# A graph network's edge loop: the bias laid into PSUM by ScalarE, half of the one-hot matrices made on GpSimd, and a new order of the stages

## The reference

```
h    = relu(layernorm(x))                        # 3125 x 256
ei   = concat([h[src], edge_attr])               # 50000 x (256 + 64)
core = relu(ei @ W1 + b1) @ W2 + b2              # W1: 320 x 256, W2: 256 x 256
gate = sigmoid(ei @ Wg + bg)                     # Wg: 320 x 256
msg  = gate * core                               # 50000 x 256
agg  = segment_sum(msg, dst, 3125)
x    = x + layernorm(agg + h) * gamma + beta
```

## Time and profile before

| | |
|---|---|
| median of three runs | 1698.13 us (1695.11 to 1700.46) |
| span of the profiled execution | 1691.9 us |
| busy: TensorE matmul, weight load | 1511.9 us (89%), 1378.6 us (81%) |
| busy: VectorE, ScalarE, GpSimd | 1469.6 us (87%), 1202.7 us (71%), 1036.2 us (61%) |
| DMA | mean 188 GB/s |

### The profile page before, as it was taken

The page is one execution under the profiler, slowest core; times in us unless marked ns, Lnnn a source line. Parts: engine busy times, 40 slices in busy tenths (PEclk is TensorE's granted clock), DMA queues, the critical chain, the costliest instruction groups (busy, mean ns, idle before and its releaser), DMA issues. The chain is left out here.

```text
span 1691.9 us, 40433 instructions
## 1 busy us (share of the span) xinstructions
PE 1511.9 (89%) x10735; PEld 1378.6 (81%) x10735; DVE 1469.6 (87%) x3257; ACT 1202.7 (71%) x2896; POOL 1036.2 (61%) x1093
## 2 busy tenths in 40 slices
PE   6879999999999999999669688999998999999874
PEld 3669999999999999999459567787787887777653
DVE  4559999999999999999577689999999999999866
ACT  1458888888888888888056367777776767777573
POOL 0446666666666666664176577777777777777316
PEclk9989999999999999999979899999999999999888
DMA  4356666666666666665125787777777777777813
GB/s 135 138 184 186 187 186 186 186 187 186 187 187 188 185 188 185 187 184 145 33 82 191 221 245 220 231 228 231 227 228 224 225 229 227 229 226 223 281 46 97
DMA packets 164893, 318.92 MB, mean 188 GB/s; under 512 B 30231, under 2 KB 103928, under 8 KB 164436
## 3 DMA queue, kind: packets, MB, share of 16 engines
q0 software_dynamic: 66560, 219.06, 44.8%
q1 hardware_dynamic: 98132, 97.49, 18.7%
HBM read 291.90 MB, written 24.53 MB: 187 GB/s over the span
## 5 line engine op out<-in xcount | busy, mean ns | idle before, releaser
L493 POOL DMA_INDIRECT gath<-edge_in_tab,idx x392 | 413.6, 1055 | 270.5 <-DVE gate_in L933 207.6
L1226 PE MATMUL bank<-weighted,hot 128*128 128x260 f32 x880 | 238.6, 395 | 30.7 <-ACT hot L749 29.6
L506 POOL DMA_INDIRECT kept_more<-kv_tab,idx x176 | 195.5, 1111 | 60.6 <-issue 39.3
L1226 PE MATMUL bank<-w_lo,relu_hi 128*128 128x256 f32 x784 | 221.8, 283 | 0.0
L1226 PE MATMUL bank<-w_hi,relu_lo 128*128 128x256 f32 x784 | 221.7, 283 | 0.0
L1226 PE MATMUL bank<-w_hi,relu_hi 128*128 128x256 f32 x784 | 221.1, 282 | 0.0
L1226 PEld LDWEIGHTS bank<-weighted,hot 128*128 128x128 f32 x880 | 153.2, 192 | 53.4 <-ACT hot L749 36.7
L644 ACT ACTIVATE relu_hi<-bank 128x512 fp32r<-128x512 f32 x196 | 117.4, 599 | 81.4 <-PE bank L1226 81.4
L506 POOL DMA_INDIRECT hs<-kv_tab,idx x132 | 148.1, 1122 | 41.3 <-issue 36.3
L506 POOL DMA_INDIRECT xs<-kv_tab,idx x132 | 141.0, 1068 | 48.7 <-issue 22.7
L1229 PE MATMUL bank<-ident,gath 128*128 128x128 f32 x784 | 150.1, 273 | 10.6 <-DMA gath<-edge_in_tab,idx 10.6
(11 more groups left out here) (284 smaller groups left out, 4924.4 us busy)
## 6 DMA issues: line engine op xcount, KB each, us to landing
block_row<-row_tab SPq DMA_DIRECT2D x440, 64.0 KB
ea_in<-in_ea SPq DMA_DIRECT2D x392, 64.0 KB, 2.4
edge_in_tab<-node_row SPq DMA_DIRECT2D x26, 256.0 KB, 2.0
kv_tab<-qkv_row SPq DMA_DIRECT2D x25, 258.0 KB, 2.5
gath<-edge_in_tab,idx POOLq DMA_INDIRECT x392
xs<-in_x SPq DMA_DIRECT2D x1, 3328.0 KB, 15.2
v_in<-kv_tab SPq DMA_DIRECT2D x25, 130.0 KB, 2.1
rows_tab<-hs SPq DMA_DIRECT2D x25, 128.0 KB, 2.4
```

Source lines behind the costliest of these rows:

```text
L493: g.indirect_dma_start(gath[:, q, i, :], None, edge_in_tab, bass.IndirectOffsetOnAxis(ap=idx[:, half, q, i:i + 1], axis=0)).then_inc(gath_ ...
L506: g.indirect_dma_start(kept(u, 0, KVW)[:, i, :], None, kv_tab, bass.IndirectOffsetOnAxis(ap=idx1[:, half, u % BATCH, i:i + 1], axis=0)).th ...
L1226: return nc.tensor.matmul(out_, lhsT=lhs, rhs=rhs, start=start, stop=stop)
```

## The change

1. b2 is loaded as `b2_rows`, 128 partitions of two copies. A new ScalarE stage `seed` copies it into the bank of `core`; `core` has 12 products instead of 14, all of which accumulate.
2. The one-hot matrices of odd blocks are made on GpSimd by `odd_one_hot`, with an is-equal. ScalarE makes those of even blocks.
3. GpSimd's gathers are written out for all chunks, with the indices straight from `src_chunk`; `idx` and its copy go.
4. VectorE's order: `low_relu`, `add_gate`, `message`, `low_edges`, `low_message`, `add_sums`; lags of sums and low messages are one more, on TensorE too. On ScalarE `gates` is ahead of `high_message`.
5. `split_edges` and `low_edges` work on two chunks at a time, in even steps; `load_edges` waits accordingly. The gate's products wait for `gate_added`.
6. In the prologue, semaphores are merged (same waits), b2's split goes, and one load is added.

```diff
@@ sync
-            sp.dma_start(b2_sb[:], b2.to_broadcast([2 * SHARES, HID])).then_inc(w_in, 16)
+            for i in range(2):
+                sp.dma_start(b2_rows[:, i, :], b2.to_broadcast([P, HID])).then_inc(w_in, 16)
...
-                after(sp, ea_lo_done, c - SLOTS + 1)
+                after(sp, ea_lo_done, (c - SLOTS) // 2 + 1)
@@ gpsimd
+            def gather_node_rows(c):
+                after(pool, gate_added, c - SLOTS + 1)
                 for i in range(2):
+                    g.indirect_dma_start(gath[:, c % SLOTS, i, :], None, edge_in_tab,
+                                         bass.IndirectOffsetOnAxis(ap=src_chunk[:, c, i:i + 1], axis=0)).then_inc(gath_in[c % SLOTS], 16)
+            def odd_one_hot(b):
+                if b % 2 == 1:
+                    after(pool, sum_ready, b - 1)
+                    for i in range(2):
+                        last = g.tensor_scalar(hot[:, 1, i, :], iota_node[:], rel_col[:, b, i:i + 1], None, ALU.is_equal)
+                    last.then_inc(pool_hot_done, 1)
...
+            chunks_and_blocks(pool, [(gather_node_rows, 0, CHUNKS), (odd_one_hot, 4, CHUNKS)])
@@ scalar
             def split_edges(c):
+                if c % 2:
+                    return
...
+                act.wait_ge(ea_arrived[slot + 1], 32 * (c // SLOTS + 1))
+                after(act, z_ready, c + 1 - SLOTS + 1)
+                after(act, gate_ready, c + 1 - SLOTS + 1)
+                s.copy(ea_parts[:, slot:slot + 2, :], ea_in[:, slot:slot + 2, :]).then_inc(ea_hi_done, 1)
...
+            def seed(n):
+                if n < 2:
+                    act.wait_ge(row_ready, WPAD)
+                after(act, msg_done, n - 1)
+                s.copy(bank[4 + n % 2][:], b2_rows[:].rearrange("p i f -> p (i f)")).then_inc(seeded, 1)
             chunks_and_blocks(act, [(split_edges, 0, CHUNKS), (one_hot, 4, CHUNKS), (distances, 3, CHUNKS), (relu_inner, 2, CHUNKS),
-                                    (high_message, 4, CHUNKS), (gates, 3, CHUNKS)])
+                                    (gates, 3, CHUNKS), (high_message, 4, CHUNKS), (seed, 2, CHUNKS)])
@@ vector
             def low_edges(c):
+                if c % 2:
+                    return
...
+                both = slice(slot, slot + 2)
+                v.tensor_tensor(ea_parts[rows, both, :], ea_in[rows, both, :], ea_parts[rows, both, :], ALU.subtract).then_inc(ea_lo_done, 1)
...
-            chunks_and_blocks(dve, [(message, 3, CHUNKS), (low_relu, 2, CHUNKS), (add_gate, 2, CHUNKS), (low_edges, 0, CHUNKS),
-                                    (low_message, 3, BLOCKS), (add_sums, 4, BLOCKS)])
+            chunks_and_blocks(dve, [(low_relu, 2, CHUNKS), (add_gate, 2, CHUNKS), (message, 3, CHUNKS), (low_edges, 0, CHUNKS),
+                                    (low_message, 4, BLOCKS), (add_sums, 5, BLOCKS)])
@@ tensor
             def edge_inputs(c):
...
+                after(pe, gate_added, c - 1)
...
             def core(n):
+                pe.wait_ge(seeded, n + 1)
                 pe.wait_ge(relu_lo_done, n + 1)
                 for i in range(2):
-                    mm(to, share[:], b2_parts[:], True, False)
...
-            chunks_and_blocks(pe, [(edge_inputs, 0, CHUNKS), (sum_messages, 3, BLOCKS), (core, 1, CHUNKS)])
+            chunks_and_blocks(pe, [(edge_inputs, 0, CHUNKS), (sum_messages, 4, BLOCKS), (core, 1, CHUNKS)])
```

More of the change, by code:

```diff
@@ L48 @@
 assert MID[-1] == WINDOWS
[L49 removed]
+assert CHUNKS % 2 == 0 and CHUNKS % (2 * SLOTS) == SLOTS and MSGS % SLOTS == 0 and MSGS > LATE + 4 and BLOCKS % KEEP == 0 and KEEP % BROWS == 0
 def build(nc, x, src, dst, etype, ea, w1, wg, b_cat, w2, b2, ln0, query_col, wqkv, b_qkv, rel, wo, b_o, ln1, out):
@@ L657, in distances @@
             def distances(b):
[L659 to L662, removed]
-            def one_hot(b):
-                act.wait_ge(dist_done, b + 1)
-                after(act, sum_ready, b - 1)
-                s.activation(hot[:, b % 2, :, :], dist[:, b % 2, :, :], ACT.Relu, bias=one_col[:], scale=-1.0).then_inc(hot_done, 1)
+                if b % 2 == 0:
+                    after(act, hot_done, b // 2)
+                    for i in range(2):
+                        last = s.activation(dist[:, i, :], iota_node[:], ACT.Square, bias=rel_col[:, ds(b, 1), i], scale=-1.0)
+                    last.then_inc(dist_done, 1)
+            def one_hot(b):
+                if b % 2 == 0:
+                    act.wait_ge(dist_done, b // 2 + 1)
+                    after(act, sum_ready, b - 1)
+                    s.activation(hot[:, 0, :, :], dist[:], ACT.Relu, bias=one_col[:], scale=-1.0).then_inc(hot_done, 1)
+            def seed(n):
[3 more added lines that the diff above has]
+                s.copy(bank[4 + n % 2][:], b2_rows[:].rearrange("p i f -> p (i f)")).then_inc(seeded, 1)
             chunks_and_blocks(act, [(split_edges, 0, CHUNKS), (one_hot, 4, CHUNKS), (distances, 3, CHUNKS), (relu_inner, 2, CHUNKS),
-                                    (high_message, 4, CHUNKS), (gates, 3, CHUNKS)])
+                                    (gates, 3, CHUNKS), (high_message, 4, CHUNKS), (seed, 2, CHUNKS)])
             act.wait_ge(lw_in, 3 * 16)
@@ L918, in low_edges @@
             def low_edges(c):
+                if c % 2:
+                    return
                 slot = c % SLOTS
-                dve.wait_ge(ea_hi_done, c + 1)
+                dve.wait_ge(ea_hi_done, c // 2 + 1)
                 rows = slice(EDGE_DIM, 2 * EDGE_DIM)
-                v.tensor_tensor(ea_parts[rows, slot, :], ea_in[rows, slot, :], ea_parts[rows, slot, :], ALU.subtract).then_inc(ea_lo_done, 1)
+                both = slice(slot, slot + 2)
+                v.tensor_tensor(ea_parts[rows, both, :], ea_in[rows, both, :], ea_parts[rows, both, :], ALU.subtract).then_inc(ea_lo_done, 1)
             def low_relu(c):
@@ L1242, in _ @@
                 last = mm(bank[2][0:1, 0:BLOCKS], ones_c[0:HALF_C, 0:1], chosen[:, c, :], c == 0, c == 1)
-            last.then_inc(rows_ready, 1)
-            pe.wait_ge(off_ready, 1)
+            last.then_inc(tallies_made, 1)
+            pe.wait_ge(lists_made, 4)
             for i in range(2):
@@ L1269, in _ @@
                     last = mm(bank[3][0:HALF_B, cols], chosen[:, c, some], nat_f[:, 2, c, :], c == 0, c == 1)
-            last.then_inc(cols_ready, 1)
+            last.then_inc(tallies_made, 1)
             pe.wait_ge(meta_ready, 1)
-            pe.wait_ge(w_in, 9 * 16)
+            pe.wait_ge(w_in, 10 * 16)
             def transpose_rows(rows, source_done, freed, ready):
@@ L1325, in edge_inputs, with onto @@
                 last.then_inc(gate_ready, 1)
+            def onto(out_, lhs, rhs):
+                return nc.tensor.matmul(out_, lhsT=lhs, rhs=rhs, start=False, stop=False, skip_group_check=True)
             def core(n):
+                pe.wait_ge(seeded, n + 1)
                 pe.wait_ge(relu_lo_done, n + 1)
@@ L1349, in sum_messages @@
                 pe.wait_ge(msg_lo_done, b + 1)
-                pe.wait_ge(hot_done, b + 1)
+                if b % 2 == 0:
+                    pe.wait_ge(hot_done, b // 2 + 1)
+                else:
+                    pe.wait_ge(pool_hot_done, b // 2 + 1)
                 to = bank[6 + b % 2][:, 0:HID]
```

67 lines of the change are left out of this document (23 added, 44 removed).

## The result

The changed kernel takes 1644.51 us, median of four runs (1641.24 to 1649.24); beside it on the same chip the kernel before takes 1696.72 (1695.11 to 1700.46). The ratio is 0.9698, 95% interval 0.9682 to 0.9713: 52 us faster.

What follows compares the result with a forecast made beforehand. TensorE was taken to bound the first layer's loop: 192 x 0.238 = 45.7 us saved, less 1 for drain and 1 for stalls, 43.7. Span 1648.2 plus 6.2 gave 1654.4 us, range 1647 to 1682.

Steps and rivals of the forecast that it cites:

- What bounds, and the bias: First layer's loop: TensorE bounds; two bias products fewer save 0.238 us a chunk, 45.7 us over 192 chunks.
- Less 1 for the drain, and 1 for small stalls.: Taken off the 45.7 us saving: 1 us for one more step to drain, 1 us for small stalls, leaving 43.7.
- the floor of 3.29: TensorE's least time per chunk in the loop after the change, 3.29 us from 3.53; it set the range's end, 1647.
- No instruction goes; I count 0, and it is what lets 0.238 come through.: VectorE's low relu first, later sums: saves 0 itself, but longer cover for waits lets the bias saving through.
- the ring: VectorE's old order ties W2 stage, message, low relu and next W2 stage together; the change was to free low relu.
- The lead-in: GpSimd's delay before a gather behind a compare: at worst 0.99 us in the open, expected to be prepared during compares.
- rival 1: GpSimd becomes the bound, mildly: 6.7 to 6.9 us per two chunks, 1674 us; chance 0.16, including 0.03 for no change.
- Rival 4: GpSimd's compares and serial lead-ins make the kernel slower: 3.99 us a chunk, 1786 us, or 1700 and up; chance 0.07.
- The loop over the landings: Sum, odd one-hot, next gathers and their landing on GpSimd: 7.85 us against 8.03 available, so it just fits.
- Rivals 3 and 5: TensorE's waits exposed, 0.05 to 0.10 us a chunk, 1664 to 1674 us, chance 0.05; late bias copy, 1680, chance 0.04.
- Ports: GpSimd compares hold up VectorE's two-input SBUF instructions: 0.1 us per two chunks taken; as bound 1659 to 1674, chance 0.10.
- Split for two: VectorE's low split every second chunk: steps of 2.75 and 3.58 us, mean 3.17 in place of 3.31.

Runs made afterwards that it cites:

- Experiment 5: The changed kernel with b2 laid down by two products per chunk again, without ScalarE's copy into PSUM: 1690.28 us, ratio 0.9969.
- experiment 2: The kernel before with VectorE's new order and the later sums alone, ScalarE's order as before: 1691.04 us, ratio 0.9976.
- changed: The changed kernel, with the whole change against the kernel before: 1644.51 us, ratio 0.9698.
- experiment 11: The changed kernel with VectorE's order and lags, TensorE's sums and ScalarE's order as in the kernel before: 1671.57 us, ratio 0.9855.
- two repeats: The changed kernel run again twice, unaltered: 1646.03 us, ratio 0.9709, and 1646.05 us, ratio 0.9696.
- experiment 3: The changed kernel with the message ahead of low relu on VectorE again, lags kept: 1673.7 us, ratio 0.9865.
- experiment 10: The changed kernel, low relu still first, but low messages, hs adds and sums at the lags of the kernel before: 1777.72 us, ratio 1.0477.
- experiments 7 and 8: The changed kernel without GpSimd's compares after the first odd block: 1648.12 us; with one more, unread compare per odd block: 1715.19 us.
- experiment 4: The changed kernel with the edge features split one chunk at a time again, on ScalarE and VectorE: 1650.86 us, ratio 0.9729.

## Why the forecast was right in its mechanism and short in its size

**What bounds, and the bias.** Right. TensorE bounds before and after. The term was 192 x 0.238 = 45.7 us; measured, 195 x 0.230 = 44.9. Experiment 5 gives 0.227 for the two products.

**"Less 1 for the drain, and 1 for small stalls."** This step failed. It took a stretch that TensorE fills to 100% as free of stalls, and allowed for new ones. But a busy share by unions doesn't show them. The starts of the transposes do: a chunk of 3.69 in every eight, so that the mean is 3.55 and not the 3.53 read from one chunk. The order took those in (experiment 2), so the sign was wrong: 3.9 us gained, not 1 lost. The drain cost 0.0 in sum. By itself it does cost what was forecast: the tail is 0.8 us longer with the later sums in experiment 2 than in the kernel before, and 0.9 longer in changed than in experiment 11 (single executions; the tails of changed's two repeats lie within 0.3 of the first). Something else in the change gave that back, and no run shows what. Together 5.9 of the 9.2 us by which 43.7 fell short of 52.9. The range's lower end, 1647, rested on the floor of 3.29, and this held (3.300); it had no room for a kernel before that ran slower than 3.53.

**The rest of the miss.** The first five chunks gained 1.1 us more than the period explains (the order alone has that too: 15.9 us in experiment 2 against 17.1), the first transposes came 0.8 late, and 3.7 us lie behind the first layer, where executions of the same kernel differ by as much. With the term of the bias (-0.8) and those 5.9: 5.9 - 0.8 + 1.1 - 0.8 + 3.7 = 9.1. The time missed by 9.9, as the median lies 5.5 us above the profiled span here and was taken 6.2 above it. What lies behind the first layer and ahead of the loop, 2.9 of the miss, is luck, good or bad. The two repeats, at 1646.0, lie under the range too.

**"No instruction goes; I count 0, and it is what lets 0.238 come through."** The second half is right and the first half was not worked out. Without the order 25 of the 50 us are gone (experiment 11). The working compared VectorE's mean need, 3.17, with 3.29. It is the long step, 3.64 (forecast 3.58), together with what holds up the short one that had to be compared with 6.6: the ring, 3.18, in experiment 3, the wait for the high message and the register load, 3.21 on average, in experiment 11. A rival "the steps don't average" was missing. The edit also has two halves that are only good together: low relu first without the later low message makes changed 5% slower than the kernel before (experiment 10).

**GpSimd.** Two errors that partly cancelled, which is luck. The compare was taken at 0.47; alone it takes 0.61, beside VectorE's two-input instructions 0.80. The lead-in behind it was feared at up to 0.99; it is 0.16, as "the sequencer can prepare the gather" said. 6.59 per two chunks against the 6.3 taken and 6.58 available: rival 1 missed by a hair, and experiments 7 and 8 show how close it was. Rival 4 needed lead-ins of 0.99 in the open, and none came. The loop over the landings, forecast to "just fit", did: TensorE waits for no gather from 200 to 700 us.

**ScalarE.** 2.99 a chunk forecast, 2.84 measured; the copy into PSUM has a pitch of 0.52 (402.64 to 403.16), taken at 0.53. Busy near 90% was forecast, 86% is in the profile. Rivals 3 and 5, waits in the open: no such wait in the trace, and the W2 starts are 0.120 apart against 0.119.

**Ports.** The forecast put the cost on VectorE, 0.1 us of 6.43, and had the compares fall beside the low relu and the gate addition. That place was wrong. VectorE pays 0.07: the low message takes 0.75 in steps with a compare beside it and 0.68 in the others. GpSimd pays more. In changed all 152 compares from 200 to 700 us overlap a low split or low message, mean 0.80; in experiment 10 all 125 lie beside other instructions:

```profile
L491 POOL TENSOR_SCALAR hot<-iota_node,rel_col 128x128 fp32r<-128x128 f32 x125 | 75.5, 616 | 2.1
```

0.19 each, 0.38 us of the 6.60. Being beside one another isn't all of it: in experiment 5 71 compares run 0.5 us beside a low message and take 0.61, and in experiment 3 some take up to 1.17. What makes the difference stays open. The rule of the Trainium skill (GPSIMD Engine Reference, section Specifications), that the SBUF interfaces are shared and contended where VectorE's instruction has two SBUF inputs, agrees with the traces of changed and experiment 10, though those 71 compares don't show it; what the traces add is that here GpSimd pays more than VectorE.

**Split for two.** VectorE's need went up by about what was said (experiment 4: 3.332 a chunk without the split for two, where 3.31 was its floor before), and the change needs it: 5 us by the medians, 6.2 by the loops of the two traces.

## What to carry to other kernels

Look at starts over many steps, not only at busy shares: an engine at 100% hid a stall of 0.16 us in every eighth chunk. Where work comes only every second step, compare the long step plus whatever the short step can't undercut with two periods of the bound, not the means with one. In experiment 10 the low message stands in VectorE's queue close behind the message from which ScalarE has yet to make its other input; such a consumer must have other work ahead of it. Moving the low relu and not the low message cost more here than the whole change gained.

## What the runs showed of the hardware that was not expected

- A compare of 128x128 on GpSimd takes 0.61 us away from VectorE's instructions with two inputs in SBUF and, in changed, 0.80 beside them; the low message goes from 0.68 to 0.75, the low split stays at 0.69.
- A gather directly behind a compare shows 0.16 us of lead-in, behind another gather 0.30.
- TensorE kept busy with costlier products (26.47 of 28 us, granted clock 0.96) finished the tail 13 us sooner than with cheaper ones. Most of that is VectorE's low message and its register load in each block, 1.59 us against 1.07 and 1.26; with TensorE idle between, its clock also fell to 0.50.
- A register load ahead of a VectorE instruction shows where the instruction before it had to wait, as the load starts only with that one: 0.83 us from low message to hs add in the kernel before, 0.61 where the high message comes a step earlier and the load is done ahead.
- In the kernel before and in experiment 2 VectorE pauses for some 0.35 us inside a register load, each time 128 of its instructions after the last pause. Why stays open.
